# Last layers of a two-block decoder: each tile's convolution moved ahead of the cross-attention steps of batch 3

## The chip, the cores and the metric

The kernel runs on one core of a Trainium2 chip. The core has a matrix engine (TensorE, PE in the profile), a vector engine (VectorE, DVE), an engine for functions of one value (ScalarE, ACT), a general one (GpSimd, POOL) and one that issues transfers (SyncE, SP). Each works through its own list of instructions in order, and they meet at semaphores. The metric is the device time of one launch in microseconds (us), as the median of several runs. Smaller is better.

## The reference

Four sequences of 512 tokens with 128 features go through six sublayers, each with a LayerNorm ahead and its result added to the input:

```python
x = x + _L0_attn_ref(_layernorm(x), ...)     # A0: causal self-attention, 16 heads
x = x + _L0_xattn_ref(_layernorm(x), ctx, ctx, ...)   # X0: cross-attention, 77 keys
x = x + _L0_ffn_ref(_layernorm(x), ...)      # M0: 8 experts, best 2
x = x + _L1_attn_ref(_layernorm(x), ...)     # A1: self-attention, 16 heads
x = x + _L1_xattn_ref(_layernorm(x), ctx, ctx, mask, ...)   # X1: one head, 77 keys
x = x + _L1_ffn_ref(_layernorm(x), ...)      # F1
```

The change lies in the end of X1 and in F1. X1 projects the normed x to queries, scores them against 77 keys, takes a softmax and multiplies by the values. F1 is

```python
h = bit_linear(x, w1)                       # 128 -> 512, x rounded to 8 bits per token
h = depthwise_conv1d(h.transpose(0, 2, 1), conv_w, conv_b)   # 3 taps along the sequence
h = _silu(h.transpose(0, 2, 1))
return bit_linear(h, w2)                    # 512 -> 128, h rounded to 8 bits per token
```

## The kernel before

A batch is one sequence; a tile is 128 tokens, so there are NT = 16 tiles and QT = 4 per batch. The instruction list of each engine is written out by hand by functions such as `last_layers_pe(e)`, `last_layers_act(e)`, `last_layers_dve(e)` and `last_layers_pool(e)`; their order is the order on that engine. All earlier stages run before them and are the same in both kernels. When the last layers begin, the self-attention A1 has one unit left, X1 is nearly done for batches 0 to 2, and batch 3 still needs all of X1.

F1 goes tile by tile through the loop `for t in range(NT)`, as a pipeline over several engines:

- `conv_pe(t)` (L2165, L2166): first linear layer and convolution in one, three fp32 matmuls of 512 columns (two instructions each, so x6 in the profile) and one bf16 matmul for the bias, into one of three PSUM banks. It waits for the turned norm of its batch (`emptied(("normed", ...))`) and for silu of tile t-3, which frees its bank.
- `silu_act(t)` (L2173), then `quantize_dve(t)` (L2180 to L2187): largest value per token, scales, rounding; then `integer_act(t)` (L2192), which gives bf16 integers.
- `turn_h_pe(t)` (L2198): four bf16 transposes; `turned_h_act(t)` (L2204) copies them out.
- `out_pe(t)` (L2213): four bf16 matmuls, the second linear layer; `out_dve(t)` (L2220) adds the result to x.

In step t of the loop PE does `turn_h_pe(t)`, `conv_pe(t + 3)` and `out_pe(t)`.

Between them stand the steps of batch 3 of X1: `norm_pe`/`norm_act` (transposes of the normed x, L547, and their copy, L561 or L556), `cross_q_pe`/`cross_q_act` (queries, L2010), `cross_score_pe` (L2026), then on DVE and POOL the scaling, row maximum and shift, `cross_exp_act` (exponentials, L2049), `cross_turn_pe`/`cross_turn_act` (transposes of the probabilities, L2064, and their copy, L2072), `cross_out_pe` (times the values, L2080), `cross_out_act` (scaling, four instructions, L2089) and `cross_add_pool` (L2095).

Each batch of F1 needs its own norm: `moments_dve` (L469 to L475), `norm_pool` (L496), `normalise` (L490), `scales_dve` (L2136 to L2140), `integers_of` (L2145, L2149, on POOL for batch 2 and on DVE for batch 3), then `norm_pe` and `norm_act`. Batch 3's uses X1's result for batch 3, batch 2's doesn't. `conv_pe(8)`, the first of batch 2, waits for `norm_act(F1, 2)`, and `conv_pe(12)` for `norm_act(F1, 3)`.

The step of X1's batch 3 that reads the exponentials waits for them as

```python
e.wait_ge(c["probs"], b + 1)          # cross_turn_pe
bank = take_bank(e, key, out=4)
```

`take_bank` gives out PSUM banks in the order of the calls on PE; in this loop two banks take turns. On ACT, silu and the exponential need different function tables, so the profile shows a table load ahead of the first of each kind.

Of the kernel before, what the change touches and what calls it, by code (L numbers as in the profile page):

```python
# [19 lines left out]
NT = NB * QT  # L20
# [242 lines left out]
def build(nc, d, out):  # L263
# [4 lines left out]
    with es:  # L268
# [190 lines left out]
        def moments_dve(e, ln, b):  # L459

            n = norm_number(ln, b)
            if ln == 0:
                e.wait_ge(s_x[min(b, 2)], 16)
            else:
                e.wait_ge(*x_at[(ln - 1, b)])
            wait(e, s_xn, n)
            take_wait(e)
            for j in range(QT):
                e.bn_stats(stats[:, j, :], tile_of(4 * b + j)).then_inc(s_stat, 1)  # L469
            e.wait_ge(s_stat, QT * (n + 1))  # L470
            take_wait(e)
            for j in range(QT):
                e.bn_aggr(mv[:, j, :], stats[:, j, :]).then_inc(s_aggr, 1)
            e.wait_ge(s_aggr, QT * (n + 1))
            e.tensor_scalar(var[:], mv[:, :, 1], EPS, None, ALU.add).then_inc(s_var, 1)  # L475
# [63 lines left out]
        def norm_pe(e, ln, b):  # L539
            n = norm_number(ln, b)  # L540
            if ln == F1.ln:
                e.wait_ge(s_xq, b + 1)
            else:
                e.wait_ge(s_xn, n + 1)
            bank = take_bank(e, ("normed", n), out=4)
            for j in range(QT):
                i = e.transpose(bank[:, j * P:(j + 1) * P], normal(ln, b)[:, j, :], ident[:])  # L547
            i.then_inc(is_filled(("normed", n)), 1)
            turned_at[n] = filled(("normed", n))
# [1509 lines left out]
        def cross_turn_pe(e, b):  # L2059
            key = ("cross_turn", b)  # L2060
            e.wait_ge(c["probs"], b + 1)
            bank = take_bank(e, key, out=4)
            for j in range(QT):
                i = e.transpose(bank[0:SC, j * P:(j + 1) * P], x_p[:, j], ident[:])  # L2064
            i.then_inc(is_filled(key), 1)

        def cross_turn_act(e, b):
            key = ("cross_turn", b)
            e.wait_ge(*filled(key))
            if b:  # L2070
                e.wait_ge(*filled(("cross_out", b - 1)))
            e.copy(x_pT[0:SC, :], bank_of(key)[0:SC]).then_inc(is_emptied(key), 1)  # L2072

        def cross_out_pe(e, b):
            key = ("cross_out", b)
            e.wait_ge(*emptied(("cross_turn", b)))
            e.wait_ge(*emptied("cross_v"))
            bank = take_bank(e, key, out=4)
            for j in range(QT):
                i = e.matmul(bank[:, j * P:(j + 1) * P], x_pT[0:SC, j * P:(j + 1) * P], x_v[:, b], start=True, stop=True)  # L2080
            i.then_inc(is_filled(key), 1)

        def cross_out_act(e, b):
            key = ("cross_out", b)
            e.wait_ge(*filled(key))
            e.wait_ge(c["sums"], b + 1)
            wait(e, x_done["X1"], b)
            for j in range(QT):
                i = e.activation(x_o[:, j], bank_of(key)[:, j * P:(j + 1) * P], ACT.Identity, scale=x_rec[:, j:j + 1])  # L2089
            i.then_inc(is_emptied(key), 1)  # L2090
# [65 lines left out]
        def conv_pe(e, t):  # L2156
            b, j = t // QT, t % QT
            e.wait_ge(*emptied(("normed", norm_number(F1.ln, b))))
            if t < 3:
                e.wait_ge(s["probs"], exps_at(3 * UN))  # L2160
            else:
                e.wait_ge(f["silu"], t - 2)
            bank = conv_banks[t % 3]
            for tap in range(3):
                e.matmul(bank, f_xT[:, b, j * P + tap:j * P + tap + P], f_w1c[:, tap], start=(tap == 0), stop=False)  # L2165
            e.matmul(bank, onesb[:], f_cb[:], start=False, stop=True).then_inc(f["conv"], 1)  # L2166

        def silu_act(e, t):
            e.wait_ge(f["conv"], t + 1)
            if t < 3:  # L2170
                e.wait_ge(s["pv"], chunk0[3 * UN])
            wait(e, f["hm"], t - 2)
            e.activation(f_h[:, t % 3], conv_banks[t % 3], ACT.Silu).then_inc(f["silu"], 1)  # L2173
# [15 lines left out]
        def integer_act(e, t):  # L2189
            e.wait_ge(f["hm"], t + 1)  # L2190
            wait(e, f["hT"], t - 1)
            e.activation(f_hq[:, t % 2], f_hm[:, t % 3], ACT.Copy, bias=-ROUND).then_inc(f["hq"], 1)  # L2192
# [13 lines left out]
        def out_pe(e, t):  # L2206
            k = t % 2
            e.wait_ge(f["hT_out"], t + 1)
            wait(e, x_done["F1"], t - 1)
            if t < 2:  # L2210
                e.wait_ge(s["emptied"][3 - t], jobs[3 - t])
            for cc in range(FC):
                i = e.matmul(out_banks[k][:, 0:D], f_hT[:, k, cc * P:(cc + 1) * P], f_w2q[:, cc, :],  # L2213
                             start=(cc == 0), stop=(cc == FC - 1))
            i.then_inc(f["out"], 1)
# [9 lines left out]
        def last_layers_pe(e):  # L2225
            g = 3 * UN - 1
            e.wait_ge(f["taps"], 3)
            e.wait_ge(s_cb, 16 * 3 * len(part_srcs))
            cross_turn_pe(e, 2)
            last_pv_pe(e, g)  # L2230
            conv_pe(e, 0)
            cross_out_pe(e, 2)
            finish_pe(e, g)
            conv_pe(e, 1)
            merge_pe(e, A1, NB - 1)
            conv_pe(e, 2)
            for part in range(2):
                proj_pe(e, A1, NB - 1, part)
            away[2] = away[3] = OPEN
            for t in range(NT):  # L2240
                turn_h_pe(e, t)
                if t == 0:
                    norm_pe(e, X1.ln, 3)
                elif t == 1:
                    cross_q_pe(e, 3)
                elif t == 2:
                    cross_score_pe(e, 3)
                elif t == 4:
                    cross_turn_pe(e, 3)
                elif t == 5:  # L2250
                    norm_pe(e, F1.ln, 2)
                    cross_out_pe(e, 3)
                elif t == 8:
                    norm_pe(e, F1.ln, 3)
                if t + 3 < NT:
                    conv_pe(e, t + 3)
                out_pe(e, t)

        def last_layers_act(e):
            cross_turn_act(e, 2)  # L2260
            pv_out_act(e, 3 * UN - 1)
            cross_out_act(e, 2)
            silu_act(e, 0)
            merge_act(e, A1, NB - 1)
            integer_act(e, 0)
            silu_act(e, 1)
            silu_act(e, 2)
            for t in range(NT):
                turned_h_act(e, t)
                if t + 1 < NT:  # L2270
                    integer_act(e, t + 1)
                if t == 0:
                    norm_act(e, X1.ln, 3)
                elif t == 1:
                    cross_q_act(e, 3)
                elif t == 3:
                    cross_exp_act(e, 3)
                elif t == 4:
                    cross_turn_act(e, 3)
                elif t == 5:  # L2280
                    norm_act(e, F1.ln, 2)
                    cross_out_act(e, 3)
                elif t == 8:
                    norm_act(e, F1.ln, 3)
                if t + 3 < NT:
                    silu_act(e, t + 3)

        def last_layers_dve(e):
            cross_sum_dve(e, 2)
            finish_dve(e, 3 * UN - 1)  # L2290
            quantize_dve(e, 0)
            proj_dve(e, A1, NB - 1)
            moments_dve(e, X1.ln, 3)
            quantize_dve(e, 1)
            normalise(e, X1.ln, 3)
            moments_dve(e, F1.ln, 2)
            for t in range(NT):
                if t == 6:
                    moments_dve(e, F1.ln, 3)
                if t + 2 < NT:  # L2300
                    quantize_dve(e, t + 2)
                if t == 2:
                    cross_score_dve(e, 3)
                elif t == 3:
                    scales_dve(e, 2)
                elif t == 4:
                    cross_sum_dve(e, 3)
                elif t == 6:
                    normalise(e, F1.ln, 3)
                elif t == 7:  # L2310
                    scales_dve(e, 3)
                    integers_of(e, 3)
                out_dve(e, t)

        def last_layers_pool(e):
            cross_add_pool(e, 2)
# [215 lines left out]
```

## Time and profile before

| what | us |
|---|---|
| median of 3 runs | 761.88 |
| lowest and highest of these | 761.59, 763.45 |
| the profiled execution, its own time | 766.63 |
| its span in the trace | 764.9 |
| PE busy in the span | 645.7 |
| DVE busy | 563.5 |
| ACT busy | 431.0 |
| POOL busy | 305.0 |

The span runs from the first to the last instruction of the trace; times of rows count from its start. The last layers' loop begins near 699.8 us. A row of a timeline gives the start and the length of a group of instructions; in square brackets stands how long the engine was idle ahead of it and what ended the wait. Matmuls overlap, so the step from the start of one group to the start of the next says more than the length of a group.

### The profile page before, as it was taken

Reading aid. Unit: us, or ns where it says so; the run is one execution under the profiler, and the core shown is the slowest. Engines: PE = TensorE matmul, PEld = TensorE weight load, DVE = VectorE, ACT = ScalarE, POOL = GpSimd, SP = SyncE. Lnnn points to the kernel's source line nnn. Section 1 sums busy time; section 2 is a strip of 40 time slices with the busy share of each in tenths; the row PEclk is TensorE's granted clock in tenths of the full one; section 3 lists DMA queues with packets and bytes.
Section 4 is the critical chain, followed back from the end, with each engine's and each line's share of the span. In section 5 each row is a group of like instructions: output and inputs, shape, how many; then the busy total and the mean of one; then the engine's idle time right before and its main releaser. Section 6 shows DMA issues by size and latency. Waiting matters only on the chain.

```text
span 764.9 us, 16027 instructions
## 1 busy us (share of the span) xinstructions
PE 645.7 (84%) x5015; PEld 354.0 (46%) x5020; DVE 563.5 (74%) x1664; ACT 431.0 (56%) x825; POOL 305.0 (40%) x536
## 2 busy tenths in 40 slices
PE   5679998999978887239997987899999989897987
PEld 2344454444434444239997885133323323234543
DVE  6977688687737786747776686899998898924564
ACT  1415565566665654025664454478887777884644
POOL 6653454545551335723332354275251341421310
PEclk9867998999988999559999898599999999999998
DMA  7744564453233311211113126210413110000000
GB/s 229 253 162 146 174 197 142 127 179 99 75 87 85 110 45 67 78 36 47 50 47 92 35 72 213 98 57 30 139 51 116 30 55 30 2 1 1 15 15 28
DMA packets 72802, 67.17 MB, mean 88 GB/s; under 512 B 14560, under 2 KB 67232, under 8 KB 72720
## 3 DMA queue, kind: packets, MB, share of 16 engines
q1 hardware_dynamic: 69920, 61.21, 25.9%
q0 software_dynamic: 2272, 4.69, 1.9%
q8 instruction: 42, 0.69, 0.4%
q14 instruction: 40, 0.33, 0.1%
q10 hardware_dynamic: 528, 0.26, 0.1%
HBM read 37.74 MB, written 28.00 MB: 86 GB/s over the span
## 4 chain that ended last, share of the span: by engine, by line
PE 54%; DVE 23%; issue 9%; POOL 5%; ACT 4%; DMA 3%; SPq 1%; DVEq 0%; ACTq 0%; POOLq 0%
DVE mx L614 13%; PE bank_pv L761 11%; PE bank_turn L598 7%; PE bank_scores L2165 5%; PE bank_scores L713 4%; PE bank_scores L1897 4%; PE bank_turn L1897 4%; PE bank_scores L1905 4%; PE bank_turn L780 3%; POOL routed_tokens L1858 3%; DVE stats L469 2%; PE bank_turn L602 1%; DVE xn L490 1%; PE bank_turn L822 1%; ACT probs L734 1%
## 5 line engine op out<-in xcount | busy, mean ns | idle before, releaser
L614 DVE TENSOR_REDUCE mx<-bank_turn 128x1 f32<-128x512 f32 (+4 forms) x438 | 251.3, 612 | 45.7 <-PE bank_turn L602 29.6
L713 PE MATMUL bank_scores<-stk 64*128 64x512 bf16 (+3 forms) x576 | 172.6, 363 | 4.2 <-ACT probs L734 3.0
L598 PE MATMUL bank_turn<-stk 64*128 64x77 bf16 (+4 forms) x694 | 151.3, 305 | 27.8 <-DVE mx L614 18.7
L738 ACT ACTIVATE probs<-bank_scores 128x1024 f32<-128x1024 f32 (+4 forms) x160 | 116.8, 768 | 94.8 <-PE bank_scores L713 93.7
L734 ACT ACTIVATE probs<-bank_scores 128x512 f32<-128x512 f32 x256 | 139.1, 605 | 33.9 <-PE bank_scores L713 33.1
L761 PE MATMUL bank_pv<-probs,vsl 128*32 128x512 f32 (+3 forms) x1152 | 139.3, 556 | 2.9 <-POOL probs L746 1.8
L598 PEld LDWEIGHTS bank_turn<-stk 64*128 64x128 bf16 x694 | 52.0, 98 | 123.9 <-DVE mx L614 58.0
L746 POOL TENSOR_SCALAR_AFFINE_SELECT probs<-probs 128x256 f32<-128x256 f32 x128 | 51.6, 407 | 75.2 <-ACT probs L738 73.5
L1874 POOL DMA_INDIRECT expert_outputs<-probs,y_at x39 | 37.9, 972 | 95.4 <-DVE y_at L1754 61.3
L713 PEld LDWEIGHTS bank_scores<-stk 64*128 64x128 bf16 x576 | 45.8, 94 | 27.5 <-ACT probs L734 15.4
L496 POOL TENSOR_TENSOR rstd<-var,mhalf 128x4 f32<-128x4 f32 x24 | 24.7, 1028 | 78.3 <-DVE var L475 77.9
L614 DVE TENSOR_REDUCE mx<-bank_scores 128x1 f32<-128x512 f32 x73 | 49.7, 680 | 8.0 <-PE bank_scores L598 7.7
L602 PE MATMUL bank_turn<-masked_key,later_key 64*128 64x64 bf16 x512 | 51.3, 201 | 0.0
L602 PEld LDWEIGHTS bank_turn<-masked_key,later_key 64*128 64x128 bf16 x512 | 46.0, 103 | 11.3 <-issue 3.1
L2165 PE MATMUL bank_scores<-f_w1c,w 128*128 128x512 f32 x96 | 46.1, 618 | 0.4 <-ACT w L556 0.4
L1897 PE MATMUL bank_scores<-probs,w_now 128*128 128x128 f32 x304 | 41.9, 287 | 5.4 <-DVE probs L1753 5.4
L1905 PE MATMUL bank_scores<-w,oT 128*128 x312 | 42.9, 282 | 1.6 <-DVE probs L1774 1.6
L1897 PE MATMUL bank_turn<-probs,w_now 128*128 128x128 f32 x320 | 42.9, 284 | 0.0
L1897 PEld LDWEIGHTS bank_scores<-probs,w_now 128*128 128x128 f32 x304 | 39.5, 203 | 5.8 <-DVE probs L1753 5.7
L1897 PEld LDWEIGHTS bank_turn<-probs,w_now 128*128 128x128 f32 x320 | 40.9, 201 | 0.1
L1905 PEld LDWEIGHTS bank_scores<-w,oT 128*128 128x128 f32 x312 | 39.1, 197 | 2.3 <-issue 2.3
L761 PEld LDWEIGHTS bank_pv<-probs,vsl 128*32 128x32 f32 x1152 | 23.2, 109 | 33.3 <-issue 25.7
(310 smaller groups left out, 1062.6 us busy)
## 6 DMA issues: line engine op xcount, KB each, us to landing
stk<-stack_A SPq DMA_DIRECT2D x64, 256.0 KB, 3.1
w<-in_M_w SPq DMA_DIRECT2D x12, 512.0 KB, 4.4
stack_A<-parts SPq DMA_DIRECT2D x12, 384.0 KB, 2.7
stack_A<-fill SPq DMA_DIRECT2D x8, 512.0 KB, 5.0
stk<-stack_X SPq DMA_DIRECT2D x16, 256.0 KB, 2.7
stack_A<-parts SPq DMA_DIRECT2D x12, 256.0 KB, 3.1
probs<-routed_tokens SPq DMA_DIRECT2D x39, 65.0 KB, 1.9
stack_A<-parts SPq DMA_DIRECT2D x12, 128.0 KB, 2.9
```

The source lines that it names most:

```text
L598: mm = e.matmul(o, stk[r, slot, 0, pp, qt * P:(qt + 1) * P], stk[r, slot, 1, pp, 0:keys], start=True, stop=not a.causal)
L602: mm = e.matmul(o[:, qt * P + HR * k:qt * P + HR * (k + 1)], later_keys(j, k), masked_keys(j), start=False, stop=k == 1)
L614: e.tensor_reduce(o.rearrange("p h q -> p q h"), bank_of((g, m))[:, 0:k * keys].rearrange("p (q h k) -> p q h k", q=len(tiles), h=len(hs)) ...
L713: mm = e.matmul(score_bank(g, kt, i)[:, 0:S - q0], stk[r, slot, 1, pp, kt * P:(kt + 1) * P], stk[r, slot, 0, pp, q0:S], start=True, stop=True)
L734: e.activation(probs[:, probs_of(g, kt), j + 2 * pp], score_bank(g, kt, i), ACT.Exp, scale=1 / math.sqrt(HD)).then_inc(s["probs"], 1)
L738: e.activation(probs[0:a.kp, probs_of(g, kt), j:HG:2, 0:n], bank_scores[0:a.kp, 2 * j:2 * j + 2, 0:n], ACT.Exp, scale=1 / math.sqrt(HD)).t ...
L746: e.affine_select(out=o, in_=o, compare_op=ALU.is_ge, fill=0.0, base=0, pattern=[[0, 2], [1, P]], channel_multiplier=-1).then_inc(s["maske ...
L761: mm = e.matmul(bank_pv[VW * h:VW * (h + 1), q0:S], vsl[:, slot, kt, h, :], probs[:, probs_of(g, kt), h, 0:S - q0], start=(kt == 0), stop= ...
L1874: e.indirect_dma_start(scr_y, bass.IndirectOffsetOnAxis(ap=y_at[:, t:t + 1], axis=0), y_sb[:, t % 2], None).then_inc(m["stored"][t % 2], 16)
L1897: mm = e.matmul(hid[t % 2][z][:, c * P:(c + 1) * P], w_now[:, t % 2, o:o + P], x_inT[:, t % 2], start=True, stop=True)
L1905: mm = e.matmul(y_bank[:, 0:D], act[:, t % 2, c * P:(c + 1) * P], w2[:, bass.ds(ex[t], 1), c, :].rearrange("p o n -> p (o n)"), start=(c = ...
L2165: e.matmul(bank, f_xT[:, b, j * P + tap:j * P + tap + P], f_w1c[:, tap], start=(tap == 0), stop=False)
```

## The change

In each step of the loop `conv_pe(t + 3)` goes directly behind `turn_h_pe(t)` (behind `cross_turn_pe(3)` in step 4), and the X1 steps of batch 3 behind it; the norms' transposes go behind `out_pe(t)`. `cross_out_pe(3)` and `norm_pe(F1, 2)` move from step 5 to step 4. On ACT `silu_act(t + 3)` likewise goes ahead of batch 3's steps except `cross_turn_act(3)`, and `cross_out_act(3)` and `norm_act(F1, 2)` move to step 4, in that order. On DVE `moments_dve(F1, 3)` is written at the end of step 5 in place of the beginning of step 6. POOL's and SP's lists are untouched.

```diff
@@ -2239,22 +2239,23 @@
             away[2] = away[3] = OPEN
             for t in range(NT):
                 turn_h_pe(e, t)
-                if t == 0:
-                    norm_pe(e, X1.ln, 3)
-                elif t == 1:
+                if t == 4:
+                    cross_turn_pe(e, 3)
+                if t + 3 < NT:
+                    conv_pe(e, t + 3)
+                if t == 1:
                     cross_q_pe(e, 3)
                 elif t == 2:
                     cross_score_pe(e, 3)
                 elif t == 4:
-                    cross_turn_pe(e, 3)
-                elif t == 5:
+                    cross_out_pe(e, 3)
+                out_pe(e, t)
+                if t == 0:
+                    norm_pe(e, X1.ln, 3)
+                elif t == 4:
                     norm_pe(e, F1.ln, 2)
-                    cross_out_pe(e, 3)
                 elif t == 8:
                     norm_pe(e, F1.ln, 3)
-                if t + 3 < NT:
-                    conv_pe(e, t + 3)
-                out_pe(e, t)
 
         def last_layers_act(e):
             cross_turn_act(e, 2)
@@ -2269,6 +2270,10 @@
                 turned_h_act(e, t)
                 if t + 1 < NT:
                     integer_act(e, t + 1)
+                if t == 4:
+                    cross_turn_act(e, 3)
+                if t + 3 < NT:
+                    silu_act(e, t + 3)
                 if t == 0:
                     norm_act(e, X1.ln, 3)
                 elif t == 1:
@@ -2276,14 +2281,10 @@
                 elif t == 3:
                     cross_exp_act(e, 3)
                 elif t == 4:
-                    cross_turn_act(e, 3)
-                elif t == 5:
+                    cross_out_act(e, 3)
                     norm_act(e, F1.ln, 2)
-                    cross_out_act(e, 3)
                 elif t == 8:
                     norm_act(e, F1.ln, 3)
-                if t + 3 < NT:
-                    silu_act(e, t + 3)
 
         def last_layers_dve(e):
             cross_sum_dve(e, 2)
@@ -2295,8 +2296,6 @@
             normalise(e, X1.ln, 3)
             moments_dve(e, F1.ln, 2)
             for t in range(NT):
-                if t == 6:
-                    moments_dve(e, F1.ln, 3)
                 if t + 2 < NT:
                     quantize_dve(e, t + 2)
                 if t == 2:
@@ -2311,6 +2310,8 @@
                     scales_dve(e, 3)
                     integers_of(e, 3)
                 out_dve(e, t)
+                if t == 5:
+                    moments_dve(e, F1.ln, 3)
 
         def last_layers_pool(e):
             cross_add_pool(e, 2)
```

## Rows read from the trace of the kernel before

**Rows 1.** The page, its part on busy time of each engine.

```profile
PE 645.7 (84%) x5015; PEld 354.0 (46%) x5020; DVE 563.5 (74%) x1664; ACT 431.0 (56%) x825; POOL 305.0 (40%) x536
```

**Rows 2.** Chain of waits in order of time: start us, us, what.

```profile
739.00 0.88 DVE w L2149 x4
```

**Rows 3.** Timeline of PE from 686 us: start, us, instructions, idle before.

```profile
699.78 0.39 PE L2198 MATMUL bank_pv<-identb,parts 128*128 128x128 bf16 x4
704.78 0.72 PE L547 MATMUL bank_turn<-ident,xn 128*128 128x128 f32 x4 [4.61 <-DVE xn L490]
705.29 4.42 PE L2165 MATMUL bank_scores<-f_w1c,w 128*128 128x512 f32 x6
709.76 0.39 PE L2213 MATMUL bank_scores<-f_w2q,parts 128*128 128x128 bf16 x4
...
710.21 1.08 PE L2010 MATMUL bank_turn<-xnT,X_wq 128*128 128x512 f32 x2
711.12 2.74 PE L2165 MATMUL bank_scores<-f_w1c,w 128*128 128x512 f32 x6
...
721.84 0.61 PE L2064 MATMUL bank_turn<-ident,w 128*77 128x128 f32 x4
722.29 2.74 PE L2165 MATMUL bank_scores<-f_w1c,w 128*128 128x512 f32 x6
...
725.97 1.06 PE L2080 MATMUL bank_turn<-x_v,w 77*128 77x128 f32 x8
727.41 2.84 PE L2165 MATMUL bank_scores<-f_w1c,w 128*128 128x512 f32 x6 [0.39 <-ACT w L556]
...
737.12 0.39 PE L2198 MATMUL bank_pv<-identb,parts 128*128 128x128 bf16 x4
739.92 0.66 PE L547 MATMUL bank_turn<-ident,w 128*128 128x128 f32 x4 [2.42 <-DVE w L2149]
...
743.66 2.79 PE L2165 MATMUL bank_scores<-f_w1c,w 128*128 128x512 f32 x6
...
746.50 0.39 PE L2213 MATMUL bank_turn<-f_w2q,parts 128*128 128x128 bf16 x4
```

**Rows 4.** Busy time by engine, PE clock, DMA share and GB/s, in four stretches.

```profile
706.00:707.00 1.00, 1.00 (x2) 0.34 (x1) 0.93 (x6) 0.12 (x1) 0.57 (x1) 0.50 0.00 0
709.00:710.00 1.00, 0.95 (x7) 0.43 (x7) 0.00 (x0) 0.04 (x1) 1.00 (x2) 1.00 0.00 0
740.00:742.00 2.00, 2.00 (x8) 1.18 (x9) 1.65 (x6) 0.58 (x1) 0.00 (x0) 1.00 0.42 128
760.00:761.00 1.00, 0.46 (x4) 0.19 (x2) 0.12 (x1) 0.51 (x1) 0.00 (x0) 0.50 0.00 0
```

**Rows 5.** Timeline of ACT from 686 us.

```profile
721.21 0.46 ACT L2049 ACTIVATE w<-x_lg 128x308 f32<-128x308 f32 x1
721.69 1.28 ACT L2173 ACT_TABLE_LOAD   x1
722.98 0.60 ACT L2173 ACTIVATE probs<-bank_scores 128x512 f32<-128x512 f32 x1
...
726.77 0.59 ACT L556 COPY w<-bank_turn 128x512 f32<-128x512 f32 x1
727.24 1.16 ACT L2089 ACTIVATE w<-bank_turn,x_rec 128x128 f32<-128x128 f32 x4
...
737.09 0.60 ACT L2173 ACTIVATE probs<-bank_scores 128x512 f32<-128x512 f32 x1 [1.69 <-PE bank_scores L2166]
737.59 0.59 ACT L2204 ACTIVATE parts<-bank_pv 128x512 bf16<-128x512 bf16 x1
...
740.62 0.58 ACT L556 COPY w<-bank_turn 128x512 f32<-128x512 f32 x1 [1.92 <-PE bank_turn L547]
```

**Rows 6.** Timeline of POOL from 686 us.

```profile
721.71 1.41 POOL L2145 TENSOR_SCALAR w<-w,f_scale 128x128 f32<-128x128 f32 x4 [3.62 <-DVE f_scale L2140]
```

**Rows 7.** Timeline of ACT from 480 us, the second stream's first table load.

```profile
486.63 1.28 ACT L734 ACT_TABLE_LOAD   x1 [17.31 <-PE bank_scores L713]
```

## The prediction

> **What bounds the kernel now.** I read the page's busy shares first: TensorE (PE) is busy for 84% of the span, more than any other engine [rows 1]. A share over the whole span says nothing of one stage, so I went on to the chain of waits, read in order of time. The change touches only the last layers, and there the chain runs on PE from 687 us to 757 us, nearly all of it convolutions. It leaves PE, before the closing tiles, for the LayerNorm of cross-attention's batch 3, for a copy by ScalarE (ACT) before tile 8's convolution, and for the quantized norm of F1's batch 3, whose last piece, on DVE, is in [rows 2].
>
> Then I read PE's timeline over that stretch [rows 3]. Here is what to see.
>
> - The convolution of tile 12 starts at 743.66 with nothing waited for. From 743.66 to the next `out_pe` at 746.50 is 2.84 us. A small group of four bf16 matmuls takes a step of 0.22 (709.76 to 710.21 is `out_pe` plus `turn_h_pe`, 0.45). A tile without cross-attention is thus 3.29 us of PE.
> - PE stops at 700.00 (`turn_h_pe` of tile 0 began at 699.78) and resumes at 704.78, when DVE has written `xn`: 4.78 us.
> - The convolution behind that hole (tile 3) takes 705.29 to 709.76 = 4.47 us in place of 2.84. [...] That costs 1.63.
> - Tile 8's convolution starts at 727.41. `cross_out_pe` started at 725.97 and needs a step of 0.9 (that of `cross_q_pe`, 710.21 to 711.12, of the same matmul duration), so 0.55 is waiting.
> - PE waits in tile 8 from 737.12 + 0.22 = 737.34 to 739.92: 2.58 us.
>
> **The change part by part.** No instruction is added or removed, no DMA is touched, SP's queue is as before, and so is POOL's order. On DVE, `moments_dve` of F1's batch 3 stands behind `out_dve(5)` and ahead of `quantize_dve(8)` in both versions: the same instruction order, 0 us. The rest is order on PE and ACT. I therefore write the new timeline of PE from the steps above.
>
> *Tiles 0 to 3.* `conv_pe(3)` needs the silu of tile 0 and the norm of batch 0, both old by then, so it starts at 700.00 and fills the hole: `out_pe(0)` at 702.85, PE free at 703.07. `norm_pe` of batch 3 still starts at 704.78, since DVE's chain up to `xn` is ahead of everything moved. The hole is now 1.71. Then, with step 0.50 for the norm (704.78 to 705.29): `turn_h_pe(1)` 705.28, conv 4 at 705.50, `cross_q_pe` 708.35, `out_pe(1)` 709.25, conv 5 at 709.70, `cross_score_pe` 712.55, `out_pe(2)` 713.45, conv 6 at 713.90, `out_pe(3)` 716.75, `turn_h_pe(4)` 716.97, done at 717.20. ACT and DVE follow: ACT's norm copy of batch 3 ends near 706.1, long before `cross_q_pe`; DVE's quantize steps stay one to two tiles ahead. Before, `cross_turn_pe` started at 721.84 and `turn_h_pe(4)` 0.22 earlier, so this part is worth 721.62 - 716.97 = **4.65 us** (3.07 of idle and 1.6 of clock). If the clock would not fall in an unprofiled run of before, 3.0.
>
> *The exponential, tile 3 to 4.* This is the price. `cross_turn_pe(3)` needs the exponentials. Before, ACT did them ahead of `silu_act(6)`, and they ended at 721.67, just ahead of PE's 721.84 [rows 3, 5]. Now ACT has them behind `silu_act(6)`, which waits for conv 6. From the end of a convolution to silu is 0.20 (conv 11 ends at 737.12 - 0.23 = 736.89, silu starts 737.09), silu takes 0.60, the load of exp's table 1.28 with 0.01 to 0.02 around it, the exponential 0.46 [rows 5]. So 716.75 + 0.20 + 0.60 + 1.31 + 0.46 = 719.32, and PE goes on at about 719.37. New wait: 719.37 - 717.20 = **2.17 us**. What is late next: `cross_turn_pe`, and conv 7 behind it (719.82, step 0.45), and with these all that follows. POOL's integers of batch 2, two passes of 1.4 that began at 721.71 [rows 6], wait for DVE's `scales_dve(2)`, which comes behind tile 5's quantize and so some 4 us earlier now: done near 720.8, while `norm_pe` asks for them at 723.79. They aren't late.
>
> *Tile 4 to 5.* Conv 7 ends at 722.67; `cross_out_pe` 0.90, `out_pe(4)` at 723.57, `norm_pe` of F1's batch 2 at 723.79, `turn_h_pe(5)` 724.29, free at 724.51. Conv 8 needs the copy `norm_act`, which on ACT now stands behind `silu_act(7)` and `cross_out_act(3)`. And `silu_act(7)` needs its table back. Does that load run early, while ACT waits for conv 7, or after the wait? Elsewhere a load begins when PE's result is there: ACT idles 17.31 us, PE's scores end that, and only then the load starts [rows 7]. So: 722.67 + 0.20 + 1.29 = 724.16 silu, a step of 0.50 (737.09 to 737.59), four scalings 1.16 less an overlap of 0.12 (726.77 + 0.59 against 727.24), copy 0.59, release 0.05 [rows 5]: conv 8 at **726.34**. Before 727.41, a gain of 1.07 is left. Bounds: with an early load 0.9 more (PE's own norm result, filled at 724.49 by the 0.70 from 739.92 to 740.62, then doesn't bind either); nothing in the rows makes it later than this.
>
> *Tile 8.* From conv 8 to `turn_h_pe(8)` nothing changes: 727.41 to 737.12 = 9.71, so 736.05. Now conv 11 follows at once (736.27), `out_pe(8)` 739.12, `norm_pe` 739.34. DVE finished the integers at 739.00 + 0.88 = 739.88 [rows 2]; its stretch starts with `out_dve(5)`, 1.07 earlier now, so 738.81: in time by 0.53. ACT's copy starts 0.70 behind `norm_pe`, takes 0.58 and 0.05, so conv 12 starts at 740.67, where PE alone would be ready at 740.06 (0.61 of waiting in place of 2.58). Before 743.66: **2.99 us** gained. Tiles 9 to 15 and the closing tiles have the same order and the same steps.
>
> **Sum.** +4.65 - 2.17 - 1.28 (wait before conv 8: 1.83 for 0.55) - 0.18 (small differences of steps) + 1.97 = 2.99 us. The profiled execution is 766.63 us with a span of 764.9, and would come to 763.6. The median of the runs shown is 761.88, 4.75 lower than the profiled one; I take the same 3.0 off it: **758.9 us**, 0.39% less.
>
> [...] The trace has 1.28 for a table load and 1.31 from the end of the exponential to the next silu (721.67 to 722.98), so a switch costs 1.3 here [rows 5]. [...]
>
> **The rivals.**
>
> - *The silu table is loaded while ACT waits for conv 7.* Gain 3.9, 758.0 us. Against it is the load that came only after PE's scores [rows 7].
> - *F1's batch 3 norm isn't ready at 739.34.* The margin is 0.53, on an engine with no idle time in that chain. If DVE is late by its whole earlier margin and PE waits as before, the last 1.97 is lost but for a few tenths: gain about 1.1, 760.8 us.
> - *The clock falls in a new hole.* The hole of 2.17 (717.2 to 719.4) is close to one of 2.58 that left the clock at 1.00 and shorter than 4.78, after which it was 0.50; but in the closing tiles, where PE is busy for 0.46 of a microsecond with small holes between, it is 0.50 too [rows 4], so work around a hole counts as well. One convolution at the low clock costs 1.6: gain 1.4, 760.5 us.
> [...]
> - *Slower: the low clock stays.* The hole at 717.2 is followed by one of 1.83 at 724.5. If the clock falls in the first and these keep it down over convs 7 to 10, four times 1.6 makes 6.4 against 3.0: 765.3 us. It decides from the second such convolution (3.2 us). Against it: at 709 us it was back behind one convolution [rows 4].
> - *The move does nothing*, because conv 3 waits for something else at 700.0, or a wait I have not seen takes it back: gain 0 to 2.
>
> **How the numbers follow.** My forecast 0.60, early load 0.08, late norm 0.08, one fall of the clock 0.11, drain 0.03, slower by the clock 0.03, nothing or an unseen wait 0.07. The likeliest gives 758.9. The range goes from the early load (757.4, with half a microsecond below it) to the cases that end near no change (761.0). What a measurement of this kernel can tell from no change is 0.3%, 2.3 us, so faster means below 759.6: the forecast is 0.7 inside, and its own steps are uncertain by half of that. Faster: most of the forecast's 0.60 (0.54) and the early load, 0.62. Same: 0.33. Slower: 0.05.
>
> **What would show it.** In the profile of the changed kernel: conv 3 right behind `turn_h_pe(0)`, 2.84 long, granted clock 1.00; a hole of 1.7 before the norm's transposes; a hole of 2.2 before `cross_turn_pe`, ended by ACT's exponential; conv 8 waiting 1.8 for ACT's copy; no hole in front of tile 8's transposes, and 0.6 before conv 12; silu's table load starting behind conv 7's end. Wrong would be: a low clock anywhere from 700 to 745, a hole of over 0.2 in front of `norm_pe` of batch 3 in tile 8, or the load at 720.7.

## The result and the profile after

The changed kernel took 758.33 us (median of 20 runs, 753.26 to 760.57), the kernel before 762.14 us in the same series (20 runs, 757.59 to 767.47). The ratio is 0.9937, 95% interval 0.9912 to 0.9962: faster by 0.63%, between 2.9 and 6.7 us. Taken off the 761.88 us of the prediction, 0.63% gives 757.1. The direction was right and the gain larger than the 3.0 us forecast; 757.1 lies just below the range's 757.4.

The profiled execution of the changed kernel has a span of 757.3 us. This is 7.6 less than before's 764.9, but 3.15 of it is already there when `turn_h_pe(0)` starts (696.63 for 699.78), in front of all that was changed, and is the spread of the earlier stages. So from here on I count from the start of `turn_h_pe(0)`, and to the start of the last `out_pe`: 61.37 us before (699.78 in [rows 3], and 761.15 for the last `out_pe`) and 57.13 after (696.63 and 753.76, below). The last layers are shorter by **4.24 us**.

Busy time of the engines, from the page of the changed kernel, against [rows 1]: DVE, ACT and POOL are within about half a microsecond of what they were. PE's is 6.1 less, but 4.2 of that lies ahead of `turn_h_pe(0)`, where the kernels are the same; conv 3 has 1.6 of the rest.

```profile
PE 639.6 (84%) x5015; PEld 350.5 (46%) x5020; DVE 563.0 (74%) x1664; ACT 431.0 (57%) x825; POOL 305.2 (40%) x536
```

PE's timeline of the changed kernel from 686 us, which answers to [rows 3]:

```profile
696.63 0.39 PE L2198 MATMUL bank_pv<-identb,parts 128*128 128x128 bf16 x4
696.86 2.79 PE L2165 MATMUL bank_scores<-f_w1c,w 128*128 128x512 f32 x6
...
699.70 0.39 PE L2213 MATMUL bank_scores<-f_w2q,parts 128*128 128x128 bf16 x4
701.63 0.66 PE L547 MATMUL bank_turn<-ident,xn 128*128 128x128 f32 x4 [1.54 <-DVE xn L490]
702.12 0.39 PE L2198 MATMUL bank_pv<-identb,parts 128*128 128x128 bf16 x4
...
713.71 0.39 PE L2198 MATMUL bank_pv<-identb,parts 128*128 128x128 bf16 x4
716.10 0.66 PE L2064 MATMUL bank_turn<-ident,w 128*77 128x128 f32 x4 [2.01 <-ACT w L2049]
716.60 2.74 PE L2165 MATMUL bank_scores<-f_w1c,w 128*128 128x512 f32 x6
719.40 1.05 PE L2080 MATMUL bank_turn<-x_v,w 77*128 77x128 f32 x8
...
720.96 0.39 PE L2198 MATMUL bank_pv<-identb,parts 128*128 128x128 bf16 x4
722.16 2.84 PE L2165 MATMUL bank_scores<-f_w1c,w 128*128 128x512 f32 x6 [0.81 <-ACT w L556]
...
735.16 0.61 PE L547 MATMUL bank_turn<-ident,w 128*128 128x128 f32 x4
735.60 0.39 PE L2198 MATMUL bank_pv<-identb,parts 128*128 128x128 bf16 x4
736.44 2.84 PE L2165 MATMUL bank_scores<-f_w1c,w 128*128 128x512 f32 x6 [0.45 <-ACT w L556]
...
753.76 0.40 PE L2213 MATMUL bank_turn<-f_w2q,parts 128*128 128x128 bf16 x4 [0.69 <-ACT parts L2204]
```

Read it by steps. Conv 3 starts behind `turn_h_pe(0)`, is 2.79 long instead of 4.42, and the hole ahead of the norm's transposes is 701.63 - 699.92 = 1.71. The hole ahead of `cross_turn_pe` is 716.10 - 713.93 = 2.17, ended by ACT's exponential (L2049). The row gives it as 2.01 idle, since a group ends a little later than the step to the next would have it; I call it the hole of 2.0 us below. Before conv 8 it is 722.16 - 721.18 = 0.98. In tile 8 `norm_pe` starts at 735.16 with no idle time in front, and conv 12 waits 736.44 - 735.82 = 0.62.

The granted clock in five stretches of the changed kernel (PE, PEld, DVE, ACT and POOL busy, PE clock, DMA share, GB/s), against [rows 4]:

```profile
697.00:700.00 3.00, 3.00 (x12) 1.27 (x10) 2.81 (x16) 0.60 (x1) 0.87 (x1) 1.00 0.00 0
702.00:705.00 3.00, 3.00 (x13) 1.46 (x13) 2.81 (x15) 1.36 (x3) 1.61 (x2) 1.00 0.00 0
714.00:716.00 2.00, 0.09 (x2) 0.00 (x0) 1.76 (x8) 1.97 (x4) 1.42 (x5) 1.00 0.21 65
716.00:718.00 2.00, 1.90 (x8) 1.18 (x9) 0.89 (x3) 1.98 (x5) 1.63 (x4) 1.00 0.24 71
718.00:720.00 2.00, 1.95 (x10) 1.17 (x10) 0.00 (x0) 1.22 (x2) 0.00 (x0) 1.00 0.03 8
```

It is 1.00 in all of these, behind the first hole and behind the second.

ACT's timeline of the changed kernel, against [rows 5]:

```profile
713.68 0.60 ACT L2173 ACTIVATE probs<-bank_scores 128x512 f32<-128x512 f32 x1 [1.73 <-PE bank_scores L2166]
714.30 1.28 ACT L2049 ACT_TABLE_LOAD   x1
715.59 0.46 ACT L2049 ACTIVATE w<-x_lg 128x308 f32<-128x308 f32 x1
...
716.95 0.57 ACT L2072 COPY w<-bank_turn 77x512 f32<-77x512 f32 x1
717.54 1.28 ACT L2173 ACT_TABLE_LOAD   x1
719.60 0.60 ACT L2173 ACTIVATE probs<-bank_scores 128x512 f32<-128x512 f32 x1 [0.78 <-remote]
720.49 1.14 ACT L2089 ACTIVATE w<-bank_turn,x_rec 128x128 f32<-128x128 f32 x4 [0.30 <-PE bank_turn L2080]
721.50 0.60 ACT L556 COPY w<-bank_turn 128x512 f32<-128x512 f32 x1
```

Exp's table load starts behind silu 6 (713.68 + 0.60), as predicted. But silu's load (717.54) starts at the end of the copy ahead of it (716.95 + 0.57), 1.9 us before conv 7 ends, and lies hidden under conv 7. ACT then waits with the table loaded, and silu 7 runs at 719.60, 0.20 behind conv 7's end. That is where I was wrong.

### The profile page after: what moved, and what is told of

The parts are those of the page before. It is cut to its first block, busy times and chain, and to the rows that moved or that the text cites. A ratio compares the mean times of both kernels' runs of the same rounds, so it can differ in the third digit from the quotient of the medians.

```text
span 757.3 us, 16027 instructions
## 1 busy us (share of the span) xinstructions
PE 639.6 (84%) x5015; PEld 350.5 (46%) x5020; DVE 563.0 (74%) x1664; ACT 431.0 (57%) x825; POOL 305.2 (40%) x536
## 4 chain that ended last, share of the span: by engine, by line
PE 54%; DVE 22%; issue 9%; POOL 5%; ACT 4%; DMA 3%; SPq 1%; DVEq 0%; ACTq 0%; POOLq 0%
DVE mx L614 13%; PE bank_pv L761 11%; PE bank_turn L598 7%; PE bank_scores L2165 5%; PE bank_scores L713 4%; PE bank_scores L1897 4%; PE bank_turn L1897 4%; PE bank_scores L1905 4%; POOL routed_tokens L1858 3%; PE bank_turn L780 3%; DVE stats L469 2%; PE bank_turn L602 2%; DVE xn L490 1%; PE bank_turn L822 1%; ACT probs L734 1%
```

## The experiments

All figures of the last layers below count from the start of `turn_h_pe(0)`. Where the last column is empty, the kernel was executed once and only its trace is used; the ratios are of medians.

| kernel | conv 4 | conv 7 | conv 8 | conv 12 | last `out_pe` | ratio to before, interval |
|---|---|---|---|---|---|---|
| before | 11.34 | 22.51 | 27.63 | 43.88 | 61.37 | |
| changed | 5.71 | 19.97 | 25.53 | 39.81 | 57.13 | 0.9937, 0.9912 to 0.9962 |
| changed, second execution | 5.71 | 19.97 | 25.53 | 39.81 | 57.13 | |
| changed, third execution | 5.71 | 20.25 | 27.22 | 41.50 | 58.82 | |
| late load | 5.72 | 19.98 | 28.15 | 42.43 | 59.75 | |
| late load, again | 5.71 | 19.98 | 28.15 | 42.43 | 59.76 | |
| warm hole | 9.64 | 20.81 | 25.93 | 42.18 | 59.61 | |
| tile 0 alone | 7.29 | 18.45 | 23.58 | 39.82 | 57.10 | 0.9947, 0.9913 to 0.9982 |
| tile 8 alone | 11.97 | 23.13 | 28.26 | 42.54 | 59.86 | |
| exp first | 5.71 | 17.75 | 23.38 | 37.66 | 54.99 | 0.9905, 0.9868 to 0.9941 |
| norm first | 5.71 | 20.40 | 26.21 | 40.44 | 57.76 | |
| exp and norm first | 5.71 | 17.75 | 22.85 | 37.08 | 54.61 | 0.9884, 0.9837 to 0.9931 |
| two convs | 3.30 | 16.91 | 22.04 | 36.27 | 53.59 | 0.9878, 0.9829 to 0.9928 |

**Late load.** Theory: the order in which an activation's waits are written decides when its table load starts; the load doesn't wait for what is written first, but for what is written behind it. `silu_act` writes its wait for the convolution first, and its load (717.54) came 1.9 us before conv 7's end. The exponential whose load in [rows 7] did wait for the scores has another wait, for `pv`, written ahead of that one. The edit writes another wait first for tile 7:

```diff
         def silu_act(e, t):
+            if t == 7:
+                e.wait_ge(f["hm"], t - 2)
             e.wait_ge(f["conv"], t + 1)
```

> The changed kernel with one wait of tile 7's silu written ahead of its wait for the convolution, so that the wait for conv 7 stands ahead of the table load. Theory A (the position of the load among the waits decides when silu's table comes back): the load starts at conv 7's end, conv 8 starts 0.9 us later against tile 0's transposes than in the changed kernel (26.4 us behind them in place of 25.5), and so does all behind it. Theory B (ACT loads a table whenever it is free, wherever the wait stands): conv 8 stays at 25.5 us.

ACT's timeline of this kernel, and PE's:

```profile
719.32 0.57 ACT L2072 COPY w<-bank_turn 77x512 f32<-77x512 f32 x1
723.69 1.28 ACT L2175 ACT_TABLE_LOAD   x1 [3.80 <-issue]
724.98 0.60 ACT L2175 ACTIVATE probs<-bank_scores 128x512 f32<-128x512 f32 x1
```

```profile
718.47 0.66 PE L2064 MATMUL bank_turn<-ident,w 128*77 128x128 f32 x4 [2.01 <-ACT w L2049]
718.97 4.44 PE L2165 MATMUL bank_scores<-f_w1c,w 128*128 128x512 f32 x6
...
727.14 2.84 PE L2165 MATMUL bank_scores<-f_w1c,w 128*128 128x512 f32 x6 [1.74 <-ACT w L556]
```

The load now starts at 723.69, behind conv 7's end, and the wait ahead of conv 8 is 1.74 in place of the changed kernel's 0.81: 0.93 more, as my sum had it. Theory A holds for silu and B falls: the order of the two waits decides when this load starts, 723.69 behind the convolution in place of 717.54 ahead of its end. Why it does isn't shown.

One load of the kernel before doesn't follow from that order. It stands ahead of the silu of M0, the experts, whose activation has a single wait written right ahead of it, for PE's result, and yet the load came behind that result:

```profile
340.57 1.28 ACT L1945 ACT_TABLE_LOAD   x1 [10.64 <-PE bank_turn L1897]
```

This activation, unlike the others, reads its bias at an index that is only known while the kernel runs. Whether that moves the wait was not tested.

Conv 8 came later still, though, at 28.15 and not 26.4: conv 7 took 4.44 in place of 2.74, because here the clock fell behind the 2.0 us hole (0.65 at 719 to 720 us, 0.50 from 720 to 722). This was my third rival, and it asked for a count.

> The kernel with the late table load once more. The wait before conv 8 is 1.7 us again in place of 0.8, whatever the clock does. If the clock holds, conv 8 starts 26.4 us behind tile 0's transposes, 0.9 later than in the changed kernel; if it falls, 28.1 again.

The same again: 1.74 us of waiting, conv 8 at 28.15, conv 7 at the low clock (0.50 from 713 to 716 us, 4.44 long). Neither execution of this kernel had the clock holding, so the 26.4 was not seen; but against an execution of the changed kernel in which the clock fell too (the third, below, 27.22) conv 8 is again 0.93 later.

**The clock behind the second hole.** Two more executions of the changed kernel itself:

> The changed kernel once more, for the granted clock behind the hole of 2.0 us ahead of the transposes of the probabilities. In the first profile the clock stayed at 1.00 there; in two variants with the same hole it fell. If the fall depends only on when the hole comes, it falls in some executions of the changed kernel too, with 1.3 to 1.6 us more in the last layers (58.4 to 58.8 in place of 57.1 from tile 0's transposes to the last output matmul). If the variants' own edits caused it, it never falls here.

> The same, a third execution of the changed kernel: 57.1 or 58.4 to 58.8 us, by the clock behind the hole.

The first of these has 57.13, the clock staying at 1.00. The other has 58.82, 1.69 more. Its granted clock in three stretches, and PE's groups at that place:

```profile
710.00:711.00 1.00, 0.01 (x1) 0.02 (x1) 0.93 (x5) 0.99 (x3) 0.89 (x4) 1.00 0.50 152
...
712.00:713.00 1.00, 1.00 (x2) 0.43 (x2) 0.00 (x0) 0.98 (x2) 0.52 (x2) 0.50 0.00 0
713.00:714.00 1.00, 1.00 (x2) 0.34 (x1) 0.00 (x0) 0.88 (x1) 0.00 (x0) 0.50 0.00 0
```

```profile
710.99 0.98 PE L2064 MATMUL bank_turn<-ident,w 128*77 128x128 f32 x4 [2.01 <-ACT w L2049]
711.76 4.16 PE L2165 MATMUL bank_scores<-f_w1c,w 128*128 128x512 f32 x6
...
718.73 2.84 PE L2165 MATMUL bank_scores<-f_w1c,w 128*128 128x512 f32 x6 [0.82 <-ACT w L556]
```

The hole is the same, ended by the same exponential at the same distance (19.48 behind `turn_h_pe(0)`), but the clock goes to 0.50 while the transposes run, and conv 7 pays: 4.16 in place of 2.74, behind transposes of 0.98 in place of 0.66. Over all profiles with this hole (three of the changed kernel, two with the late load, one with the norm first) it fell in four of six. So the changed kernel's gain in its last layers is 4.24 us in some executions and 2.55 in others, against the one trace of before. Of the changed kernel itself it fell in one of three, and two traces more with the same instructions up to the hole (the late load) had it: what share of the timed runs it is, six traces can't say.

**Warm hole.** Did the low clock behind the first hole really cost 1.6 us? The kernel before, with a convolution's matmuls issued once more into the bank that conv 3 overwrites:

```diff
                 if t == 0:
+                    e.wait_ge(f["silu"], 1)
+                    for tap in range(3):
+                        e.matmul(conv_banks[0], f_xT[:, 0, tap:tap + P], f_w1c[:, tap], start=(tap == 0), stop=(tap == 2))
                     norm_pe(e, X1.ln, 3)
```

> The kernel before with the three matmuls of a convolution issued once more, for nothing, in the 4.8 us hole ahead of batch 3's transposes; conv 3 then overwrites the bank. Nothing else moves. If the low clock behind the hole costs what I took (1.6 us), conv 3 takes 2.8 us in place of 4.4 at a granted clock of 1.00 and the last layers, from tile 0's transposes to the last output matmul, take 59.8 us in place of 61.4. If conv 3 was slow for another reason, it stays at 4.4 us.

PE's timeline there, and two stretches with the clock:

```profile
693.50 2.79 PE L2245 MATMUL bank_scores<-f_w1c,w 128*128 128x512 f32 x6
698.28 0.65 PE L547 MATMUL bank_turn<-ident,xn 128*128 128x128 f32 x4 [1.98 <-DVE xn L490]
698.77 2.74 PE L2165 MATMUL bank_scores<-f_w1c,w 128*128 128x512 f32 x6
```

```profile
697.00:698.00 1.00, 0.00 (x0) 0.00 (x0) 1.00 (x5) 0.63 (x1) 0.00 (x0) 1.00 0.00 0
...
700.00:702.00 2.00, 2.00 (x13) 1.01 (x12) 1.29 (x6) 0.24 (x1) 1.89 (x2) 1.00 0.00 0
```

Conv 3 takes 2.74, and the last layers 59.61: 1.76 less, with more work and nothing moved. 1.70 of it is there at conv 4 (9.64 for 11.34), 0.06 comes in the closing tiles.

**Tile 0 alone.** The kernel before with only step 0 changed:

```diff
                 turn_h_pe(e, t)
                 if t == 0:
+                    conv_pe(e, 3)
+                    out_pe(e, 0)
                     norm_pe(e, X1.ln, 3)
-                elif t == 1:
+                    continue
+                if t == 1:
                     cross_q_pe(e, 3)
```

(and on ACT `silu_act(e, 3)` ahead of `norm_act`.)

> The kernel before with tile 0's part of the change alone (conv 3, its silu and output ahead of batch 3's norm). By my sum this part alone is worth 4.65 us: the exponential stays ahead of silu 6, so nothing is given back. From tile 0's transposes to the last output matmul 56.7 us in place of 61.4; median faster by 0.6%. The rival, that a shift so early is eaten by a later wait that the whole change happens to avoid, would leave 2 us or less.

57.10: 4.27 us less. At conv 8 it is 4.05 (23.58 for 27.63), and the 0.6 that is missing to 4.65 is visible: `cross_q_pe`, with conv 4 not in front of it here, starts 0.61 behind the end of `turn_h_pe(1)`, held by ACT's copy (0.45 of idle time in its row). The other 0.22 of the 4.27 comes in the closing tiles, where one group ran at the low clock in the trace of before (0.50 at 760 to 761 us in [rows 4]). This one move gives as much as the whole change at its best, 57.13; by the medians the two can't be told apart, since the intervals of their ratios overlap.

**Tile 8 alone.** The kernel before with `norm_pe(F1, 3)` behind `out_pe(8)`, and `norm_act` behind `silu_act(11)`:

```diff
-                elif t == 8:
-                    norm_pe(e, F1.ln, 3)
                 if t + 3 < NT:
                     conv_pe(e, t + 3)
                 out_pe(e, t)
+                if t == 8:
+                    norm_pe(e, F1.ln, 3)
...
```

> The kernel before with tile 8's part of the change alone (batch 3's F1 transposes behind conv 11 and the output, its copy behind silu 11). My sum gives 1.97 us: no hole in front of the transposes, 0.6 in front of conv 12, and 59.4 us from tile 0's transposes to the last output matmul in place of 61.4. The rival of my prediction, DVE late with the integers, would leave a hole in front of the transposes.

The last `out_pe` is at 59.86, but conv 3 had a longer piece of the low clock in this execution (0.50 from 699 to 703 us; conv 3 took 4.65 for 4.42, the transposes ahead of it 1.11 for 0.72, and conv 4 comes at 11.97 for 11.34); up to there the instructions are those of before, so before's own time varies by such pieces too. From conv 4 to conv 12 it is 42.54 - 11.97 = 30.57 against 43.88 - 11.34 = 32.54: 1.97 less, and no hole in front of the transposes.

**Exp first.** The exponential back in front of silu 6:

```diff
-                if t == 4:
+                if t == 3:
+                    cross_exp_act(e, 3)
+                elif t == 4:
                     cross_turn_act(e, 3)
                 if t + 3 < NT:
...
-                elif t == 3:
-                    cross_exp_act(e, 3)
                 elif t == 4:
                     cross_out_act(e, 3)
```

> The changed kernel with the exponential of batch 3 back ahead of silu 6 on ACT. If the hole of 2 us ahead of the transposes of the probabilities is due to that place alone, it goes, silu 6 comes 1.3 us later for nobody, and the last layers gain 2.1 us more (55.0 us from tile 0's transposes to the last output matmul). Rival: silu 6 behind two table loads holds DVE's quantize of tile 6 or the copy before conv 8, and less than 1 us is left.

54.99, 2.14 less than the changed kernel: the hole of 2.17 is gone and nothing took its place.

**Norm first.** In step 4 `norm_pe(F1, 2)` ahead of `cross_out_pe(3)`, and `norm_act` ahead of `cross_out_act`:

```diff
                 elif t == 4:
+                    norm_pe(e, F1.ln, 2)
                     cross_out_pe(e, 3)
                 out_pe(e, t)
                 if t == 0:
                     norm_pe(e, X1.ln, 3)
-                elif t == 4:
-                    norm_pe(e, F1.ln, 2)
...
                 elif t == 4:
+                    norm_act(e, F1.ln, 2)
                     cross_out_act(e, 3)
-                    norm_act(e, F1.ln, 2)
```

> The changed kernel with the transposes and the copy of F1's batch 2 norm ahead of batch 3's last cross-attention step (PE and ACT), all in step 4. If conv 8 waits only because its copy stands behind four scalings on ACT, the wait of 0.8 us goes and conv 8 starts 24.6 us behind tile 0's transposes in place of 25.5. If it waits for POOL's integers of batch 2, the wait moves to the transposes and nothing is won.

The wait ahead of conv 8 is gone, but the clock fell behind the 2.0 us hole here too (0.50 from 714 to 717 us; the transposes at 19.47 took 1.14 in place of 0.66), and conv 8 comes at 26.21. Against the third execution of the changed kernel, where it also fell, that is 1.0 less; the two low stretches aren't equally long, so the size stays open in this run.

**Exp and norm first.**

> The changed kernel with both: exponential ahead of silu 6, norm of batch 2 ahead of the last cross-attention step. If the two holes are independent, 2.1 and 0.9 us add up: last output matmul 54.1 us behind tile 0's transposes, 3.0 less than in the changed kernel. If ACT becomes the limit (two table loads and four scalings within two tiles), less.

Conv 8 starts 0.53 earlier than with the exponential alone (22.85 for 23.38), not 0.9. PE's row says who takes the rest:

```profile
716.31 0.66 PE L547 MATMUL bank_turn<-ident,w 128*128 128x128 f32 x4 [0.53 <-POOL w L2149]
```

The transposes of batch 2's norm, asked for 3.3 us earlier than in the changed kernel (2.1 of it from the exponential), now wait for POOL's second pass of the integers. The two holes were not independent: behind them stands POOL.

**Two convs.** The same with conv 4 in step 0 as well:

```diff
-                if t + 3 < NT:
+                if t + 3 < NT and t != 1:
                     conv_pe(e, t + 3)
...
                 if t == 0:
+                    conv_pe(e, 4)
                     norm_pe(e, X1.ln, 3)
```

> The last one with conv 4 also ahead of cross-attention's batch 3 transposes (in step 0, and none in step 1), so that the remaining hole of 1.6 us is filled too. Conv 4 is 1.2 us longer than the hole and ACT's copy then lies bare for 0.6, so about 1.0 us less: 53.1 us. If the later start of batch 3 only moves the wait to its exponentials, no gain.

53.59, 1.02 less than the last; 0.2 of it is a higher clock in one group of transposes of the closing tiles (0.40 us for 0.61; 0.50 at 749 to 750 us in the last kernel, 1.00 at 748 to 749 in this one), 0.8 is the hole. Its two waits in this stretch:

```profile
703.19 1.13 PE L2010 MATMUL bank_turn<-xnT,X_wq 128*128 128x512 f32 x2 [0.45 <-ACT xnT L561]
...
715.97 0.66 PE L547 MATMUL bank_turn<-ident,w 128*128 128x128 f32 x4 [0.55 <-POOL w L2149]
```

It is the shortest of all: 7.8 us less than before in the last layers and 3.5 less than the changed kernel; its median was 753.11 us against 762.73 for before in the same series (6 and 11 runs). By the medians alone it can't be told from exp and norm first, which had 753.53.

## Why the prediction was partly wrong

- *Tiles 0 to 3*, "this part is worth 4.65 us": right. `cross_turn_pe` comes at 19.47 in place of 22.06, and with the 2.17 of the new wait that is 4.65 + 0.1. Its part of 1.6 for the clock (0.50 at 706 to 707 us, inside conv 3, in [rows 4]) was shown apart by the warm hole (1.70), and the hole shrank from 4.78 to 1.71 as said; tile 0 alone gave 4.05 at conv 8, with 0.61 of a new wait.
- *The exponential*, "new wait: 2.17 us": right to the hundredth, and undone by putting it back.
- *Tile 4 to 5*, "elsewhere a load begins when PE's result is there": this step failed. I took the load's place from one row [rows 7], of an activation whose waits are written in another order, put silu's load on the path behind conv 7, and gave the early load 0.08. In the trace the load lay hidden under conv 7. The late-load kernel shows that for silu the order in which two waits are written decides it, and the price is 0.93 us; the hole before conv 8 was 0.98, not 1.83. Conv 8 came at 25.53 behind `turn_h_pe(0)`, where the sum had 26.56.
- *Tile 8*, 0.61 before conv 12, and DVE in time: right, 0.62; tile 8 alone gave the 1.97 of the sum.
- *The sum.* 2.99 + 0.93 for the load makes 3.9, and the trace has 4.07 at conv 12 and 4.24 at the last `out_pe`; the last 0.17 doesn't come from the order of the instructions. Between the last two `out_pe`, where `turn_h_pe(15)` ran at the low clock before (0.61 for 0.40 us), the trace of before has 0.22 more; 0.05 went the other way.
- *The clock in a new hole*, a rival at 0.11: it happens, in four of six profiles with this hole, and costs 1.7. I had taken one hole of 2.4 to 2.6 us that left the clock at 1.00 as evidence for all. That the clock held in the first trace was luck. In the third it was low behind the hole, which the prediction names as a sign of being wrong.
- *The number.* The measured 0.63%, 4.8 us with an interval from 2.9 to 6.7, can't tell 4.24 from 3.1 (4.24 less four sixths of 1.7). So the load accounts for the 0.9 between 3.0 and 3.9, but not for the rest of the way to 757.1: with the trace's whole 4.24 the forecast would have been 757.6, inside the range. Why the medians differ by 4.8 and the traces by 4.24 stays open; 4.24 lies within the interval.
- *The drain*, 0.03 among the chances: no run shows one. What they show in its place is a load that starts 0.02 behind the activation ahead of it, in both directions (from silu to the exponential's load 714.28 to 714.30 in the changed kernel, from the exponential to silu's 721.67 to 721.69 in [rows 5]). The load takes 1.28, and from the end of one activation to the start of the next it is 1.31 (714.28 to 715.59, 721.67 to 722.98).

How the gain of the median divides over executions with and without the fall of the clock stays open: the trace of each timed run would be needed.

## What to carry to other kernels

An in-order engine's queue is best filled across a wait with work that is long ready: one convolution moved in front of one wait was worth as much as all the moves together (4.27 us for 4.24), because the others cost as much as they gave. Before moving a step behind another on a second engine, look at who needs it first: the exponential behind silu 6 gave back 2.2 us. And where an activation needs another function table, write the wait for the latest event first, so that the load doesn't stand behind it. That paid 0.93 us at the one place tried here, and the load at L1945 didn't follow it, so check in a row where the load starts.

## What the runs showed of the hardware

A hole in PE's work of 2.0 us, the same in six executions, was followed by the low clock (0.50) in four of them (changed, third execution; late load twice; norm first) and by 1.00 in two (changed, first and second); one such low stretch cost 1.7 us (conv 7 4.44 for 2.74), nearly as much as the hole itself. The hole's length alone doesn't decide it: the one of 2.4 us in tile 8 left the clock at 1.00 in all three traces that have it (before, 740 to 742 us; warm hole, 732 to 734; tile 0 alone, 735 to 737). What does decide it is not shown. And the same instructions ahead of the last layers took between 691.5 and 696.6 us in three executions of one kernel, so that a change of 4 us can only be sized from the trace of its stage.
